# First group's S^T as four products side by side, modulation columns and gate rows at steps 9 to 13, identity products beside the first maxima

## The reference, cut to what matters

```
c_proj = silu(c) @ W_mod + b_mod                    # shift, scale and gate, twice
x_norm = modulate(ln(x), shift_a, scale_a)
q, k, v = split(x_norm @ W_qkv + b_qkv)
attn = softmax(q @ k^T * scale)                     # 2 samples x 16 heads, 512 x 512
x = x + gate_a * ((attn @ v) @ W_proj + b_proj)
...                                                 # cross attention, MLP with shift_m, scale_m, gate_m
```

## Time and profile before

| | |
|---|---|
| median of three runs | 461.62 us (460.95 to 465.91) |
| the profiled execution, its span | 460.53 us, 458.7 us |
| PE busy, DVE busy, ACT busy | 82%, 65%, 45% of the span |
| mean granted clock of PE | 0.851 |
| steps 0 to 3, with Q, K and V of sample 1 | 17.35 to 39.62 us |
| steps 4 to 6 | 39.62 to 53.49 us |
| steps 7 to 10 | 53.49 to 75.87 us |

### The profile page before, as it was taken

The page is one execution under the profiler, slowest core; times in us unless marked ns, Lnnn a source line. Parts: engine busy times, 40 slices in busy tenths (PEclk is TensorE's granted clock), DMA queues, the critical chain, the costliest instruction groups (busy, mean ns, idle before and its releaser), DMA issues.

```text
span 458.7 us, 8982 instructions
## 1 busy us (share of the span) xinstructions
PE 374.1 (82%) x3317; PEld 210.5 (46%) x3317; DVE 297.2 (65%) x1279; ACT 204.3 (45%) x303; POOL 111.9 (24%) x130
## 2 busy tenths in 40 slices
PE   3999899999989987899888889978574566675985
PEld 2325412223333155677655567754353344454454
DVE  4648556999897056666338361235989999997342
ACT  1311126666756935666432123332453555653511
POOL 5332304910010011001015100011434544444010
PEclk9965659999999999999999585566877877776999
DMA  7544625110000000000000000000000000000000
GB/s 201 37 157 120 186 59 156 53 55 2 3 1 2 0 1 1 1 2 1 1 1 2 4 1 7 3 3 1 1 1 1 2 2 1 1 1 1 1 24 24
DMA packets 13247, 12.88 MB, mean 28 GB/s; under 512 B 2373, under 2 KB 11681, under 8 KB 13203
## 3 DMA queue, kind: packets, MB, share of 16 engines
q1 hardware_dynamic: 13007, 12.28, 10.3%
q0 software_dynamic: 160, 0.01, 0.0%
q10 hardware_dynamic: 36, 0.01, 0.0%
HBM read 9.41 MB, written 2.63 MB: 26 GB/s over the span
## 4 chain that ended last, share of the span: by engine, by line
PE 57%; DVE 29%; ACT 7%; issue 5%; POOL 1%; DMA 1%; SPq 0%; ACTq 0%; DVEq 0%; POOLq 0%
PE psum L1491 6%; PE psum L1561 5%; PE psum L1529 5%; DVE left L1284 4%; DVE left L1291 4%; PE psum L1514 4%; DVE mx L1210 4%; PE psum L1355 3%; PE psum L1660 3%; DVE top L1281 3%; DVE top L1288 3%; PE psum L1508 3%; PE psum L1485 2%; PE psum L1544 2%; PE psum L1628 2%
## 5 line engine op out<-in xcount | busy, mean ns | idle before, releaser
L1210 DVE TENSOR_REDUCE mx<-psum 128x1 f32<-128x512 f32 x128 | 81.4, 684 | 26.4 <-PE psum L1491 18.0
L803 ACT ACTIVATE big<-psum 128x1024 f32<-128x1024 f32 x64 | 62.5, 1022 | 46.1 <-PE psum L1514 25.2
L607 POOL TENSOR_TENSOR rstd<-vareps,minus_half 128x4 f32<-128x4 f32 x12 | 12.2, 1020 | 178.8 <-DVE vareps L969 178.7
L1561 PE MATMUL psum<-kblk,qf 128*128 128x308 f32 x128 | 46.0, 490 | 1.1 <-DVE qf L1157 0.8
L1572 PE MATMUL psum<-ident,pr 128*77 128x128 f32 x256 | 38.3, 299 | 10.5 <-POOL pr L725 10.5
L1491 PE MATMUL psum<-KS,QS 72*128 72x512 bf16 x112 | 43.0, 417 | 3.0 <-DVE mx L1210 2.3
L1572 PEld LDWEIGHTS psum<-ident,pr 128*77 128x77 f32 x256 | 34.4, 167 | 18.4 <-POOL pr L725 13.9
L725 POOL TENSOR_TENSOR pr<-pr,early 128x616 f32<-128x616 f32 x16 | 23.9, 1493 | 55.8 <-ACT early L909 37.8
L1529 PE MATMUL psum<-big,V 128*9 128x512 f32 x256 | 34.3, 609 | 0.5 <-ACT big L803 0.5
L1584 PE MATMUL psum<-QS,vc 77*9 77x128 f32 x256 | 13.9, 342 | 24.1 <-ACT QS L919 24.0
L1514 PE MATMUL psum<-QS,KS 75*128 75x512 bf16 x112 | 32.8, 379 | 0.4
(11 more groups left out here) (202 smaller groups left out, 687.3 us busy)
## 6 DMA issues: line engine op xcount, KB each, us to landing
QS<-scr_q SPq DMA_DIRECT2D x7, 288.0 KB
KS<-scr_k SPq DMA_DIRECT2D x7, 288.0 KB
scr_q<-qp SPq DMA_DIRECT2D x2, 384.0 KB, 2.9
scr_k<-kp SPq DMA_DIRECT2D x2, 384.0 KB, 3.6
gates<-scr_g SPq DMA_DIRECT2D x2, 320.0 KB, 4.1
early<-in_L_xcond_w_ada_dram SPq DMA_DIRECT2D x1, 576.0 KB, 5.1
scr_k<-kp SPq DMA_DIRECT2D x2, 256.0 KB, 4.3
wmlp<-in_L_xcond_W_mlp_dram SPq DMA_DIRECT2D x2, 256.0 KB, 3.2
```

The lines of the kernel that those rows point to most:

```text
L803: freed(act.activation(pT[:, u % 2, 1024 * half:1024 * (half + 1)], ps, ACT.Exp), "sT", 0, u, half)
L1210: freed(dve.tensor_reduce(mx[:, n % 3, at:at + 1], ps, AX_X, ALU.max), "max", t, q)
L1561: last = pe.matmul(ps[:, 512 * a:512 * a + HH // 2 * S], qf[:, b, i * P:(i + 1) * P], kb[:, c0:c0 + HH // 2 * S], start=True, stop=True)
```

## The change

1. The two halves of S^T of the first group (steps 7 to 10) are both made at q = 1, where they were made at q = 0 and q = 1. A function `first_halves` says which halves belong to which q.
2. The modulation columns and gate rows leave steps 4, 5 and 6: m01 goes to step 9, gate0 to 10, mods to 11, gate1 to 13, and their results to rooms of the ring Y. DVE reads them in the same steps. On SP, `spread_gates` moves from ahead of all loads of maximum rows to behind that of group 2.
3. In steps 0 to 6, PE makes one or two products ident x ident (128x128, fp32) behind each of the four tiles of maxima, 36 in all. They go to a part of W0 that nothing reads then; no semaphore hangs on them.

```diff
-EARLY = {0: ("ln",), 1: ("qk",), 2: ("v0",), 3: ("v1",), 4: ("ctx", "m01"), 5: ("kv", "gate0"), 6: ("mods", "gate1")}
+EARLY = {0: ("ln",), 1: ("qk",), 2: ("v0",), 3: ("v1",), 4: ("ctx",), 5: ("kv",), 9: ("m01",), 10: ("gate0",),
+         11: ("mods",), 13: ("gate1",)}
+BUSY = {0: 1, 1: 1, 2: 1, 3: 1, 4: 2, 5: 1, 6: 2}
...
+def first_halves(j, q):
+
+    if not 0 <= j < UNITS:
+        return ()
+    if j < NT:
+        return (0, 1) if q == 1 else ()
+    return (q,) if q < 2 else ()
...
-            spread_gates(sp)
             for n, (b, g) in enumerate(groups):
                 if n:
                     max_rows(sp, b, G * g, G, n, n % 2, s_mrow[n % 2], 3 * n)
+                if n == 2:
+                    spread_gates(sp)
...
+            def keep_clock(n):
+
+                for _ in range(n):
+                    pe.matmul(psum[:, 3 * 512:3 * 512 + P], ident[:, :], ident[:, :], start=True, stop=True)
...
                             if t < HEADS:
                                 max_L0(t, q)
-                            if q < 2 and 0 <= t - LOOK < UNITS:
-                                sT_L0(t - LOOK, q)
+                            if t in BUSY:
+                                keep_clock(BUSY[t])
+                            for half in first_halves(t - LOOK, q):
+                                sT_L0(t - LOOK, half)
```

More of the change, by code:

```diff
@@ L135, in rooms_in_turns @@
                         use("Y", "max", t, q)
-                    if q < 2 and 0 <= t - LOOK < UNITS:
-                        use("W", "sT", 0, t - LOOK, q)
+                    for half in first_halves(t - LOOK, q):
+                        use("W", "sT", 0, t - LOOK, half)
                     if q == 1 and t % G == 0 and 1 <= t // G <= B * NG:
@@ L1226, in _ @@
                             v_out(1)
-                        if t == 5:
-                            mod_out(0, 1)
                         if t == 6:
                             vc_out()
+                        if t == 9:
+                            mod_out(0, 1)
+                        if t == 10:
                             gate_rows_out(0)
+                        if t == 11:
                             mod_out(1, 0)
-                        if t == 7:
+                        if t == 13:
                             gate_rows_out(1)
```

## The result

The change takes **478.9 us** (median of four runs, 476.6 to 482.2), the kernel before 463.8 us beside it (461.0, 461.6, 465.9 and 472.5). The ratio is **1.035, 95% interval 1.024 to 1.046**: slower, as forecast, but 6 us above the 473 of the prediction, at the upper end of its range (455 to 479), with two of the four runs above it (480.1 and 482.2). One thing must be known to read these numbers: the kernel before itself takes 457 to 462 us in some of its executions and 466 to 480 us in others, and the ratio leaves the 472.5 out; the traces at the end of the experiments show where they differ.

What follows compares the result with a forecast made beforehand. PE, mostly at the low 1.2 GHz clock, was taken to bound the kernel from 17.35 to 75.87 us; +22.4 - 2.9 - 8.8 + 2.3 = +13.0 us on 460.53 gave 473.5, said as 473 us, range 455 to 479.

Steps and rivals of the forecast that it cites:

- Price of a product: Steps 0 to 3: an identity product cannot run beside a 32-row tile and costs 0.41 us at high clock, 0.73 at low.
- The third rival: Steps 0 to 3: identity products do run beside the tiles, some 16 us instead of 22.3; 444 us in all, chance 0.04.
- Level of the clock in steps 0 to 3: The clock falls in step 0 or 1 and returns only at step 4, perhaps once between, behind sample 1's Q and K.
- Steps 0 to 3: Tiles and identity products in a row, mostly at the low clock: +22.4 us, taken between +24.9 and +19.8.
- +24.9: Steps 0 to 3 with step 0 at the high clock and steps 1 to 3 all low: 47.2 us.
- The lower bound, +19.8: Steps 0 to 3 if one of steps 1 to 3 has the high clock, 5.1 us less than all three low.
- Steps 4 to 6: From 13.9 us to 11 us, start still at the low clock, identity products covered by DVE: -2.9 us.
- DVE is then the slower: Steps 4 to 6 after the change: DVE needs 10.2 us, PE 9.2 us, so DVE sets the time.
- Part 1: Steps 7 to 10, S^T side by side at the high clock: 22.4 to 13.6 us, -8.8 us, bounds -10.0 and -8.0.
- Part 2: Moved columns lengthen steps 11 and 13, where PE has no idle time: mods 1.57 and gate1 0.72, +2.3 us, at least 1.0.
- Behind step 14: From step 14 to the end: no term in the sum, so taken as unchanged, 0 us.
- The first rival, 456 us: The clock holds through steps 0 to 3, which take 28.3 us; sum -4.2, 456 us, decided in step 1; chance 0.26.

## Why the prediction was wrong in size and right in kind

Two steps of the prediction failed. It put everything from step 14 on at nothing ("the change touches only the first of these", the two slow places of the clock line), and that part was 3.1 us longer; and it took steps 0 to 3 at +22.4 where the traced execution had +24.3. The order of the products and the low clock that it forecast came as it said.

- **Price of a product: right.** 0.42 and 0.72 us (forecast 0.41 and 0.73), tile and product one behind the other, 1.47 and 2.72 us. The third rival, 444 us, is out by that; its "some 16 us" for steps 0 to 3 is also less than the 17.9 us that these steps took at least in every trace.
- **Level of the clock in steps 0 to 3: right, its reason not shown.** It fell at the end of step 0 and came back in step 4. But what was read from the earlier trace rows, that work on all rows raised the clock, does not hold from execution to execution: in the traced execution the 3.41 us of Q and K of sample 1, on 128 rows at the low level, were followed by 0.50 up to step 4, and in two traces of the kernel before the products with V left it at 0.50 through all of steps 7 to 10.
- **Steps 0 to 3: a term that was mis-sized.** "Between these I take +22.4" allowed for one step at the high level at half its weight. The profiled execution had none: +24.3 us, the end of +24.9 that was worked out and not taken. In the other two traces the high level did come back once, where the prediction said it might, for a part of a step: 43.6 us. The lower bound, +19.8, was in none of the three against the first trace of the kernel before; but that stage of the kernel before itself takes 18.05 to 24.19 us in five traces, so one trace was a loose base.
- **Steps 4 to 6: right in the number, in part by luck.** -3.2 against -2.9. But "DVE is then the slower" is not what the trace shows: PE is busy 11.22 of the 11.35 us, DVE 8.99, and the chain is PE but for 2.1 us. Nor are the products quite covered: with the clock at 1.00 the stage takes 9.69 us with them and 8.85 without. And their use was not told: they hold the clock for steps 7 to 10. Without them S^T and V lose 5.7 us (19.85 against 14.14).
- **Part 1: right at the lower bound.** -8.1 against -8.8, bounds -10.0 and -8.0. The second room was late only in step 7 (1.82 in place of 1.07 us). By itself, without the products of steps 4 to 6, the part gave -6.3.
- **Part 2: 1.6 against 2.3.** gate1 takes 0.74 us in the chain, as priced (0.72); `mods` takes 1.24 where 1.57 was taken, and 0.3 us of idle time was there to take some of it.
- **Behind step 14: the largest miss.** The prediction took this part as unchanged, for no reason that it gives. Its instructions are, but its time is not a constant: +0.4 us to the first cross score and +2.7 behind it in the profiled pair, and 295 to 303 us over all traces. What the runs show in place of the zero is a late part that moves by up to 7 us with the falls of the clock in it, in the kernel before as in the change.
- **The first rival, 456 us, fell where it said**, in step 1: when Q and K of sample 1 begin, the clock has been at 0.50 since the end of step 0. Its mechanism is real and was one product away: with two behind each tile the clock holds, and the kernel is at 459.5 us.

In this order the priced terms and the part behind step 14 missed by +1.9, -0.3, +0.7, -0.7 and +3.1 us, and the earlier start took 0.5: together 4.2 us on top of the forecast +13.0, which is the 17.2 us between the spans. The median of the runs lies another 1.2 us above the traced execution, and 473.5 was said as 473.

## What to carry to other kernels

Work added to hold a clock must not break what runs side by side: look at which rows of the array it takes and put it behind a group of narrow products, or make it as narrow as they are, not between them. Ask first whether it earns anything there: here no run shows that products in steps 0 to 3 do. With products in steps 4 to 6 only the kernel takes 452.5 us (median), with four more behind each four tiles 452.0, with narrow ones between them 451.8 and 452.0, and these are not to be told apart. Then ask of each stage by itself what the added work does there; here the same two lines lost 24 us in steps 0 to 3 and earned 6 in steps 7 to 10. And where a kernel's granted clock moves, take a second and a third trace before a stage's time is used as a price: the stage that one of these three parts shortened takes 22.3 us in three traces of the kernel before and 29.7 in two.

## What was not expected of the hardware

The granted clock can stay at 0.50 for 29.67 us in which PE is busy without a break, and the same instructions can have it back after some 14 us in another execution of the same kernel (steps 7 to 10 of the kernel before). And more work made a stage shorter: sixteen further identity products took steps 0 to 3 from 46.44 to 30.93 us.
